# A decoder layer on one core: x1's turned tiles are sent and fetched ahead of x2's second tile, and x2 is read back in four transfers instead of eight

## The chip, the cores and the metric

The kernel runs on one core of a Trainium2 chip (TensorE, called PE below; VectorE, DVE; ScalarE, ACT; GpSimd, POOL; and SyncE, SP, which here only issues transfers). The metric is the device time of one execution in microseconds (us).

## The reference

A decoder layer on x of shape (2, 2048, 512) in f32, each of its three parts followed by a layer norm over the last axis:

```python
x = layernorm(x + self_attention(x))          # linear: no softmax, so it folds to x @ M + c
x = layernorm(x + cross_attention(x, ctx))    # 16 heads of 32, 154 context keys, masked softmax
x = layernorm(x + ffn(x))                     # mixes each token with the one before it
# ffn: xr = mu_r * x + (1 - mu_r) * x_prev ; xk likewise with mu_k
#      out = sigmoid(xr @ Wr.T) * (square(relu(xk @ Wk.T)) @ Wv.T)
```

Below, x1 is the result of the first layer norm and x2 that of the second.

## The kernel before

The 4096 tokens are worked in 16 groups of 256, each of two tiles of 128 tokens. Products in f32 precision are made of three matmuls (`three_pass`, L94 to L96), since each operand is split into a high and a low half. After a prologue that folds the self attention's weights into one matrix, a software pipeline runs over passes n. The steady loop has n = 2 to 14, and in pass n the engines work on four groups at once: a = n + 1 (y product, x1, q product), n (cross attention), f = n - 1 (output product, x2, mixing) and e = n - 2 (the ffn's k, r and v products). Each engine has its own list of instructions, written out by hand in the order in which it is to do them; semaphores (`flag`) tie the lists together, and an engine whose next instruction isn't released waits, whatever stands behind it.

PE's list for a pass (L2027 to L2059) is: k_product (e, 0), transposes (n, 0, t) with o_product (f, t), y_product (a, 0 and 1), values (n, 0), scores (n, 2), k_product (e, 1), transposes (n, 1, 0), r_product (e, 0), transposes (n, 1, 1), half of r_product (e, 1), values (n, 1), scores (n, 3), the other half, transposes (n, 2, 0), v_product (e, 0), transposes (n, 2, 1), q_product (a, 0) and so on. The numbers behind n are the head group (0 to 3) and the tile (0, 1). `values` (L1841) waits for `take_turned` and `take_rest` (L897, L902), with which ACT copies the transposed weights of attention out of PSUM; `transposes` (L1819) for the second tile waits for ACT's `take_turned` of the first.

x1 and x2 come out with tokens on partitions and must be turned so that features are on partitions. DVE turns squares of 32 x 32 in place (`turn_x2`, and inside `normalise_and_turn_x1`, both L1223), which gives the `x_squares` tiles; SP sends them to a scratch tensor in DRAM (L760, L774) and reads them back from there so that the squares land on the right partitions (`fetch_x1`, L766, four transfers; `fetch_x2`, L782, eight transfers, four for each tile). The two scratch tensors have 128 rows with the pieces of both tiles. Each layer norm takes its sums on DVE, `rstd` on POOL (`scale`, L1559, a power of -0.5) and is applied on DVE (L1201 for x2, L1232 for x1).

x1's way goes on as: ACT `x1_high` (L871), DVE `x1_low` (L1244), PE q_product (a, 0). x2's way goes on as: DVE `difference` (L1293), `blend`, and the products of the next pass. After its turning work DVE does `masked_min` (n, 2, 0), which takes the scores out of PSUM and finds the row's extreme (L1256); ACT's `exponentials` (n, 2, 0) (L889) wait for it, and on ACT there follow k_high, take_turned (n, 1, 1) and take_rest (n, 1):

```python
take_turned(n, 1, 0)
exponentials(n, 2, 0)
k_high(e, 1)
take_turned(n, 1, 1)
take_rest(n, 1)
```

Of the kernel before, what the change touches and what calls it, by code (L numbers as in the profile page):

```python
# [5 lines left out]
F32 = mybir.dt.float32  # L6
# [4 lines left out]
P = 128  # L11
B, S, D = 2, 2048, 512
KT = D // P
# [6 lines left out]
GT = 256  # L20
TPG = GT // P
# [9 lines left out]
SQUARE = 32  # L31
ROWS4 = P // SQUARE
# [581 lines left out]
def layers(nc, io, mem, tile, psum, weights, kv, m_in, xt, park, fold, out):  # L614
# [12 lines left out]
    m_park, c_park, x1_park, x2_park = park  # L627
# [7 lines left out]
    LAST = NG - 1  # L635
# [10 lines left out]
    with ExitStack() as ctx:  # L646
# [77 lines left out]
        end_mm, end_gated, end_sum, end_stat = (flag(x, len(parts)) for x in ("end_mm", "end_gated", "end_sum", "end_stat"))  # L724
        end_mom, end_var, end_rstd, end_ok = (flag(x, TPG) for x in ("end_mom", "end_var", "end_rstd", "end_ok"))
        x1_out, x1_back = flag("x1_out", TPG, 16), flag("x1_back", ROWS4, 16)
        x2_out, x2_back = flag("x2_out", TPG, 16), flag("x2_back", TPG * ROWS4, 16)

        x1_high_at, x1_low_at = (lambda n, ok=ok: ok.at(2, n) for ok in (x1t_hi_ok, x1t_lo_ok))

        def sp_program(sp):
            def load_mask(n):
                if n >= 2:
                    sp.wait_ge(*s_min.at(n - 2))
                sp.dma_start(mask_in[n % 2][:], io["mask"][n * GT:(n + 1) * GT, :]
                             .rearrange("(t p) c -> p t c", p=P)).then_inc(*mask_here.up)

            def load_x(n):
                sp.wait_ge(*q_mm.at(n - 1))
                sp.dma_start(x_in[:], x_cols[:, :, n * GT:(n + 1) * GT]).then_inc(*x_here.up)  # L740

            def load_batch(b):
                sp.wait_ge(*c_parked.at(0))
                sp.wait_ge(*m_parked.at(0))
                sp.wait_ge(*y_mm.at(b * GPB - 1))
                sp.dma_start(m_raw[:], m_park.rearrange("p (k n) -> p k n", k=KT)).then_inc(*m_here.up)
                sp.wait_ge(*y_sum.at(b * GPB - 1))
                sp.dma_start(c_row[:], c_park).then_inc(*c_here.up)

            def store(n):  # L750
                sp.wait_ge(*ln_ok[3].at(n))
                sp.dma_start(out[n * GT:(n + 1) * GT, :].rearrange("(t p) d -> p t d", p=P),
                             y3[:]).then_inc(*out_kept.up)

            def send_x1(n):
                for t in range(TPG):
                    sp.wait_ge(*tr1_mm.at(n, t + 1))
                    if n > 3:
                        sp.wait_ge(*x1_back.at(n - 4))
                    sp.dma_start(x1_park.rearrange("q (j t e) -> q t j e", j=ROWS4, t=TPG)[:, t],  # L760
                                 x1_squares[t][:].rearrange("q (j e) -> q j e", j=ROWS4)).then_inc(*x1_out.up)

            def fetch_x1(n):
                sp.wait_ge(*x1_out.at(n - 3))
                for j in range(ROWS4):
                    sp.dma_start(x_in[j * SQUARE:(j + 1) * SQUARE, :, :],  # L766
                                 x1_park.rearrange("(i r) (j e) -> j r i e", i=ROWS4, j=ROWS4)[j]).then_inc(*x1_back.up)

            def send_x2(n):
                for t in range(TPG):  # L770
                    sp.wait_ge(*tr2_mm.at(n, t + 1))
                    if n > 1:
                        sp.wait_ge(*x2_back.at(n - 2))
                    sp.dma_start(x2_park.rearrange("q (j t e) -> q t j e", j=ROWS4, t=TPG)[:, t],  # L774
                                 x2_squares[t][:].rearrange("q (j e) -> q j e", j=ROWS4)).then_inc(*x2_out.up)

            def fetch_x2(n, t):
                if t == 0:
                    sp.wait_ge(*x2_out.at(n - 1))
                    sp.wait_ge(*carried.at(n))  # L780
                for j in range(ROWS4):
                    sp.dma_start(x2t[j * SQUARE:(j + 1) * SQUARE, 1 + t * ROWS4:1 + (t + 1) * ROWS4, :, :],  # L782
                                 x2_park.rearrange("(i r) (j t k s) -> j t r i k s", i=ROWS4, j=ROWS4, t=TPG, k=KT)[j, t]
                                 ).then_inc(*x2_back.up)

            def load_weight(name):
                i = late.index(name)
                if i:
                    sp.wait_ge(*w_here.at(i - 1))
                sp.dma_start(raw[name][:], io[name].rearrange("(k p) n -> p k n", p=P)).then_inc(*w_here.up)  # L790

            def park(*parts):
                i, j = parts[0], parts[-1] + 1
                sp.wait_ge(*fm_eye.at(0, j))
                sp.dma_start(m_park.rearrange("p (k n) -> p k n", k=KT)[:, i:j, :], t1[:, i:j, :]).then_inc(*m_parked.up)

            load_mask(0)
            load_weight("ffn_wk")
            sp.dma_start(bo_row[:], io["rows"][4:5, :].broadcast_to([P, D])).then_inc(*bo_here.up)
            for n in range(-1, NG + 3):  # L800
                a, f, e = n + 1, n - 1, n - 2
                if n == 1:
                    sp.wait_ge(*fc_ok.at(0))
                    sp.dma_start(c_park, fold["c_row"][:]).then_inc(*c_parked.up)
                if live(e - 1) and e - 1 < LAST:
                    store(e - 1)
                if live(f) and moved_x2(f):
                    send_x2(f)
                if live(a) and moved_x1(a):
                    send_x1(a)  # L810
                if live(f) and moved_x2(f):
                    fetch_x2(f, 0)
                if live(a) and moved_x1(a):
                    fetch_x1(a)
                if live(f) and moved_x2(f):
                    fetch_x2(f, 1)
                if live(a) and a % GPB == GPB - 1 and a + 1 < NG:
                    load_batch(batch(a) + 1)
                if live(a + 1):
                    load_mask(a + 1)  # L820
                    if n == 1:
                        park(0, 1, 2)
                    load_x(a + 1)
                if n == 1:

                    sp.wait_ge(*fm_mm.at(0))
                    park(3)
                    load_weight("ffn_wr")
                    load_weight("ffn_wv")
            sp.wait_ge(*bo_here.at(0))  # L830
            for t in range(TPG):
                row = LAST * GT + t * P
                sp.wait_ge(*end_ok.at(0, t + 1))
                sp.dma_start(out[row:row + P, :], y3[:, t, :]).then_inc(*out_kept.up)
            sp.wait_ge(*out_kept.at(LAST - 1 + TPG))
# [288 lines left out]
        def dve_program(dve):  # L1124
# [325 lines left out]
            for n in range(2, LAST):  # L1450
                a, f, e = n + 1, n - 1, n - 2
                o_low(f, 3)
                masked_min(n, 1, 0)
                masked_min(n, 1, 1)
                k_square(e, 0)
                if a == GPB:
                    next_m_low(3)
                if live(e - 1):
                    normalise(3, e - 1, y3)
                o_finish(f, 0)  # L1460
                if n == 2:
                    weight_low("ffn_wr")
                else:
                    k_low(e, 0)
                o_finish(f, 1)
                if n == 2:
                    k_low(e, 0)
                normalise(2, f, x2[f % 2])
                y_finish(a, 0)
                turn_x2(f, 0)  # L1470
                y_finish(a, 1)
                o_low(n, 0)
                turn_x2(f, 1)
                normalise_and_turn_x1(a)
                masked_min(n, 2, 0)
                k_square(e, 1)
                masked_min(n, 2, 1)
                k_low(e, 1)
                if n == 2:
                    weight_low("ffn_wv")  # L1480
                make_mask(a)
                o_low(n, 1)
                masked_min(n, 3, 0)
                x1_low(a)
                masked_min(n, 3, 1)
                difference(f)
                v_gated(e, 0)
                blend(f, "k")
                v_sums(e, 0)
                o_low(n, 2)  # L1490
                k_mix_low(f)
                masked_min(a, 0, 0)
                masked_min(a, 0, 1)
                v_finish(e, 1)
                blend(f, "r")
                carry(f + 1)
                if a == GPB - 1:
                    next_m_low(0, 1, 2)
# [614 lines left out]
def decoder_layer(nc, whole, io, out):  # L2113
# [1 line left out]

    m_park = nc.dram_tensor("m_scratch", (P, KT * D), F32, kind="Internal").ap()
    c_park = nc.dram_tensor("c_scratch", (P, D), F32, kind="Internal").ap()
    x1_park, x2_park = (nc.dram_tensor(x + "_scratch", (P, TPG * D), F32, kind="Internal").ap() for x in ("x1", "x2"))
    mem = Map(nc)
    ident = mem.place("ident", [P, P])  # L2120
    ones = mem.place("ones", [P, P])
# [89 lines left out]
```

## Time and profile before

| | |
|---|---|
| median of 3 runs | 894.3 us (893.77 to 895.22) |
| the profiled execution | 892.91 us, of which the span of the profile is 890.8 us |
| PE matmul busy | 875.6 us, 98% of the span |
| PE weight loads busy | 727.9 us, 82% |
| DVE busy | 711.5 us, 80% |
| ACT busy | 534.0 us, 60% |
| POOL busy | 499.5 us, 56% |
| TensorE clock granted | 0.999 of full |

All times in the profile are counted from the span's start. An engine's timeline gives for each instruction its start, its duration, the engine, the line of the kernel (a helper's line where a helper issues it), what it writes and reads and, in brackets, how long the engine had been idle before it and what released it. Neighbouring instructions of one engine overlap at their ends, so the distance between two starts is what one costs. The x load at the end of each pass (L740) marks the passes: pass 3 reaches from 262.83 to 308.12.

### The profile page before, as it was taken

The numbers are of one execution on the slowest core, as the hardware profiler recorded it, in microseconds if no ns is written. First come the engines' busy times: TensorE is split into PE (matmuls) and PEld (weight loads), VectorE is DVE, ScalarE is ACT, GpSimd is POOL, SyncE is SP. The second block draws the span as 40 slices with busy tenths as digits, with TensorE's granted clock in tenths as the row PEclk, the third lists the DMA queues.
The fourth block names the chain that finished last, engine by engine and source line by source line (L and its number), as shares of the span: only waits on it lengthen the run. The fifth ranks groups of instructions, "written<-read, shape, count | busy, mean of one in ns | idle before, by whom it ended". The sixth has DMA issues, their size and how long they took to land.

```text
span 890.8 us, 23143 instructions
## 1 busy us (share of the span) xinstructions
PE 875.6 (98%) x8566; PEld 727.9 (82%) x8566; DVE 711.5 (80%) x2053; ACT 534.0 (60%) x1631; POOL 499.5 (56%) x505
## 2 busy tenths in 40 slices
PE   9999999999999999999999999999999999999997
PEld 8877867778788888888888888888888888888786
DVE  6688566576898888888797878787978887977775
ACT  7555425858565757474757574757565666666631
POOL 1035014676776565666666667575757666666420
PEclk9999999999999999999999999999999999999999
DMA  9792020103412222222422222313131313130001
GB/s 293 249 276 72 24 74 26 44 2 127 126 50 88 64 82 67 80 59 87 118 79 71 72 80 66 86 61 91 61 92 57 95 50 103 48 97 25 2 24 47
DMA packets 82252, 73.80 MB, mean 83 GB/s; under 512 B 7134, under 2 KB 66526, under 8 KB 82014
## 3 DMA queue, kind: packets, MB, share of 16 engines
q1 hardware_dynamic: 78542, 65.27, 24.2%
q10 hardware_dynamic: 3600, 7.08, 2.4%
q8 instruction: 68, 1.11, 0.5%
q14 instruction: 42, 0.34, 0.1%
HBM read 47.73 MB, written 23.33 MB: 80 GB/s over the span
## 4 chain that ended last, share of the span: by engine, by line
PE 64%; POOL 8%; issue 7%; DVE 6%; ACT 1%; DMA 1%; POOLq 0%; DVEq 0%
PE dense L94 17%; PE dense L95 16%; PE dense L96 16%; PE turned L1819 5%; PE turned L1841 5%; PE scores L1805 4%; POOL row_inv L1572 2%; POOL weight L1580 2%; PE turned L1823 1%; POOL prob_rest L1579 1%; DVE stats L1188 1%; POOL x L1590 1%; POOL rstd L1559 1%; DVE x_squares L1223 1%; DMA xt_raw<-x_cols 1%
## 5 line engine op out<-in xcount | busy, mean ns | idle before, releaser
L1572 POOL TENSOR_TENSOR row_inv<-row_sum,minus_one 128x4 f32<-128x4 f32 x128 | 143.8, 1123 | 161.9 <-ACT prob L889 160.4
L889 ACT ACTIVATE prob<-prob,row_min 128x154 f32<-128x154 f32 x512 | 209.5, 416 | 17.2 <-DVE row_min L1256 17.1
L1580 POOL TENSOR_TENSOR weight<-prob,row_inv 128x512 f32<-128x512 f32 x128 | 141.0, 1102 | 0.0
L1256 DVE CUSTOM_DVE_ANT_0 prob<-scores,mask_add 128x154 f32<-128x154 f32 x512 | 128.3, 311 | 3.9 <-PE scores L1805 3.6
L897 ACT ACTIVATE prob_t<-turned 128x512 f32<-128x512 f32 x128 | 75.4, 589 | 52.5 <-PE turned L1819 52.4
L889 ACT ACTIVATION_READ_ACCUMULATOR prob<-prob,row_min 128x1 f32 x512 | 98.5, 192 | 0.0
L1819 PE MATMUL turned<-ident,weight 128*128 128x128 f32 x512 | 77.0, 273 | 2.5 <-DVE o_t_lo L1263 1.1
L94 PE MATMUL dense<-xt_hi,cross_wq_hi 128*128 128x256 f32 x256 | 76.6, 299 | 0.2 <-ACT u L846 0.2
L1819 PEld LDWEIGHTS turned<-ident,weight 128*128 128x128 f32 x512 | 61.1, 140 | 18.0 <-issue 4.1
L94 PE MATMUL dense<-mix_k_hi,ffn_wk_hi 128*128 128x256 f32 x256 | 75.1, 293 | 0.0
L95 PE MATMUL dense<-xt_lo,cross_wq_hi 128*128 128x256 f32 x256 | 73.1, 286 | 0.0
L96 PE MATMUL dense<-xt_hi,cross_wq_lo 128*128 128x256 f32 x256 | 72.6, 284 | 0.0
L910 ACT ACTIVATE o_t_hi<-turned 128x256 fp32r<-128x256 f32 x64 | 24.0, 375 | 80.3 <-PE turned L1841 80.3
L95 PE MATMUL dense<-mix_k_lo,ffn_wk_hi 128*128 128x256 f32 x256 | 71.9, 281 | 0.0
L96 PE MATMUL dense<-mix_k_hi,ffn_wk_lo 128*128 128x256 f32 x256 | 71.9, 281 | 0.0
L1559 POOL TENSOR_TENSOR rstd<-var,neg_half 128x2 f32<-128x2 f32 x47 | 35.5, 756 | 59.7 <-DVE var L1195 58.0
L1590 POOL TENSOR_TENSOR x<-x,cross_bo_row 128x1024 f32<-128x1024 f32 x16 | 38.4, 2400 | 38.2 <-DVE x_squares L1223 34.5
L1263 DVE TENSOR_TENSOR o_t_lo<-turned,o_t_hi 128x256 fp32r<-128x256 f32 x64 | 26.8, 419 | 40.0 <-ACT o_t_hi L910 39.8
L1579 POOL TENSOR_TENSOR prob_rest<-prob,row_inv 128x104 f32<-128x104 f32 x128 | 50.5, 394 | 10.0
L94 PE MATMUL dense<-cross_wo_hi,o_t_hi 128*128 128x512 f32 x128 | 53.1, 415 | 0.0
L94 PEld LDWEIGHTS dense<-mix_k_hi,ffn_wk_hi 128*128 128x128 f32 x256 | 48.2, 188 | 4.9 <-issue 4.8
L1805 PE MATMUL scores<-kt,q 32*128 32x154 f32 x1024 | 51.6, 315 | 0.0
(283 smaller groups left out, 2640.5 us busy)
## 6 DMA issues: line engine op xcount, KB each, us to landing
x_scratch<-x_squares SPq DMA_DIRECT2D x52, 256.0 KB, 2.6
x_rows<-x_rows SPq DMA_DIRECT2D x32, 256.0 KB, 4.2
xt_raw<-x_cols SPq DMA_DIRECT2D x16, 512.0 KB, 3.8
out<-gate_then_y SPq DMA_DIRECT2D x15, 512.0 KB, 2.8
x_t<-x_scratch SPq DMA_DIRECT2D x104, 64.0 KB, 2.4
xt_raw<-x_scratch SPq DMA_DIRECT2D x52, 128.0 KB, 2.8
mask_in<-mask SPq DMA_DIRECT2D x16, 154.0 KB, 2.3
cross_wv<-cross_wv SPq DMA_DIRECT2D x2, 512.0 KB, 5.3
```

Of the source, the lines that this page charges most:

```text
L94: pe.matmul(out, sta[0], mov[0], start=first, stop=False, skip_group_check=True)
L95: pe.matmul(out, sta[0], mov[1], start=False, stop=False, skip_group_check=True)
L96: return pe.matmul(out, sta[1], mov[0], start=False, stop=last, skip_group_check=True)
L889: m = act.activation(keys, keys, ACT.Exp, bias=row_min[:, buf, t, h:h + 1], scale=-1.0, accum_out=row_sum[:, buf, t, h:h + 1])
L897: act.activation(pt[:, 0:HPG, t * P:(t + 1) * P], t_bank[:].rearrange("p (c n) -> p c n", c=HPG), ACT.Copy).then_inc(*t_out.up)
L1256: m = dve.tensor_tensor_reduce(exp_slot(n, u)[:, i * CTX:(i + 1) * CTX], s_bank[:, h, t * CTX:(t + 1) * CTX], mask_add[n % 2][:, t, :], -S ...
L1572: pool.tensor_tensor(row_inv[:, buf, t, :], row_sum[:, buf, t, :], minus_one[:], ALU.pow).then_inc(*p_inv.up)
L1579: pool.tensor_tensor(after, late, inv_late, ALU.mult)
L1580: pool.tensor_tensor(first, early, inv_early, ALU.mult).then_inc(*p_norm.up)
L1590: pool.tensor_tensor(rows[:], rows[:], bo_row[:].unsqueeze(1).broadcast_to([P, TPG, D]), ALU.add).then_inc(*x1_bo.up)
L1805: m = pe.matmul(s_bank[:, h, t * CTX:(t + 1) * CTX], q[rows, g, t * P:(t + 1) * P], kt[rows, g, b * CTX:(b + 1) * CTX], start=True, stop=T ...
L1819: m = pe.transpose(t_bank[:, i * P:(i + 1) * P], weight_slot(n, u)[:, i * P:(i + 1) * P], ident[:])
```

## The change

`normalise_and_turn_x1(a)` now stands ahead of `turn_x2(f, 1)` in DVE's list. SP's list for a pass was: both tiles of x2 sent, both tiles of x1 sent, x2's first tile fetched (4 transfers), x1 fetched (4), x2's second tile fetched (4). It is now: x2's first tile sent, both tiles of x1 sent, x2's second tile sent, x1 fetched (4), x2 fetched, both tiles in each of 4 transfers of 128 KB. The scratch tensor of x2 has now a row for each token, so that each tile is sent as 128 rows of 2 KB in one piece instead of 128 x 4 pieces of 512 bytes; the reads still take pieces of 512 bytes.

```diff
-        x2_out, x2_back = flag("x2_out", TPG, 16), flag("x2_back", TPG * ROWS4, 16)
+        x2_out, x2_back = flag("x2_out", TPG, 16), flag("x2_back", ROWS4, 16)
...
-            def send_x2(n):
-                for t in range(TPG):
-                    sp.wait_ge(*tr2_mm.at(n, t + 1))
-                    if n > 1:
-                        sp.wait_ge(*x2_back.at(n - 2))
-                    sp.dma_start(x2_park.rearrange("q (j t e) -> q t j e", j=ROWS4, t=TPG)[:, t],
-                                 x2_squares[t][:].rearrange("q (j e) -> q j e", j=ROWS4)).then_inc(*x2_out.up)
-
-            def fetch_x2(n, t):
-                if t == 0:
-                    sp.wait_ge(*x2_out.at(n - 1))
-                    sp.wait_ge(*carried.at(n))
+            def send_x2(n, t):
+                sp.wait_ge(*tr2_mm.at(n, t + 1))
+                if n > 1:
+                    sp.wait_ge(*x2_back.at(n - 2))
+                sp.dma_start(x2_park[t * P:(t + 1) * P, :], x2_squares[t][:]).then_inc(*x2_out.up)
+
+            def fetch_x2(n):
+                sp.wait_ge(*x2_out.at(n - 1))
+                sp.wait_ge(*carried.at(n))
                 for j in range(ROWS4):
-                    sp.dma_start(x2t[j * SQUARE:(j + 1) * SQUARE, 1 + t * ROWS4:1 + (t + 1) * ROWS4, :, :],
-                                 x2_park.rearrange("(i r) (j t k s) -> j t r i k s", i=ROWS4, j=ROWS4, t=TPG, k=KT)[j, t]
-                                 ).then_inc(*x2_back.up)
+                    sp.dma_start(x2t[j * SQUARE:(j + 1) * SQUARE, 1:, :, :].rearrange("r b k s -> r b (k s)"),
+                                 x2_park.rearrange("(b r) (j e) -> j r b e", r=SQUARE, j=ROWS4)[j]).then_inc(*x2_back.up)
...
-                if live(f) and moved_x2(f):
-                    send_x2(f)
-                if live(a) and moved_x1(a):
+                if 2 <= n < LAST:
+                    send_x2(f, 0)
                     send_x1(a)
-                if live(f) and moved_x2(f):
-                    fetch_x2(f, 0)
-                if live(a) and moved_x1(a):
+                    send_x2(f, 1)
                     fetch_x1(a)
-                if live(f) and moved_x2(f):
-                    fetch_x2(f, 1)
+                    fetch_x2(f)
...
                 turn_x2(f, 0)
                 y_finish(a, 1)
                 o_low(n, 0)
+                normalise_and_turn_x1(a)
                 turn_x2(f, 1)
-                normalise_and_turn_x1(a)
                 masked_min(n, 2, 0)
...
-    x1_park, x2_park = (nc.dram_tensor(x + "_scratch", (P, TPG * D), F32, kind="Internal").ap() for x in ("x1", "x2"))
+    x1_park, x2_park = (nc.dram_tensor(x + "_scratch", shape, F32, kind="Internal").ap() for x, shape in (
+        ("x1", (P, TPG * D)), ("x2", (GT, D))))
```

## Rows read from the trace of the kernel before

**Rows 1.** Windows of passes 3 and 10: length, each engine's busy us, clock, DMA.

```profile
262.83:308.12 45.29, 45.29 (x496) 38.47 (x503) 38.28 (x120) 28.34 (x94) 29.44 (x31) 1.00 0.25 75
...
580.58:626.02 45.44, 45.44 (x496) 38.37 (x504) 37.83 (x119) 28.24 (x94) 29.44 (x30) 1.00 0.26 75
```

**Rows 2.** PE's waits from 232 to 810 us: total us, times, longest.

```profile
PE turned L1819 <- DVE o_t_lo L1263: 1.1, 2, 0.6
PE turned L1841 <- ACT prob_t L902: 0.9, 1, 0.9
PE dense L94 <- DVE square L1316: 0.4, 1, 0.4
```

**Rows 3.** Timeline of DVE, pass 3.

```profile
276.84 1.00 DVE L1201 TENSOR_SCALAR x<-x,moments,rstd 128x512 f32<-128x512 f32 x2 [0.81 <-POOL rstd L1559]
...
281.96 0.70 DVE L1223 STREAM_TRANSPOSE x_squares<-x 128x512 f32<-128x512 f32 x1
282.61 0.55 DVE L1232 TENSOR_SCALAR x<-x,moments,rstd 128x512 f32<-128x512 f32 x1
...
295.51 1.19 DVE L1293 TENSOR_TENSOR mix_r_raw<-x_t 128x992 f32<-128x992 f32 x1
```

**Rows 4.** Timeline of POOL, pass 3.

```profile
276.10 0.70 POOL L1559 TENSOR_TENSOR rstd<-var,neg_half 128x2 f32<-128x2 f32 x1 [3.26 <-DVE var L1195]
...
281.80 0.70 POOL L1559 TENSOR_TENSOR rstd<-var,neg_half 128x2 f32<-128x2 f32 x1
```

**Rows 5.** Timeline of ACT, pass 3.

```profile
286.04 0.42 ACT L889 ACTIVATE prob<-prob,row_min 128x154 f32<-128x154 f32 x1 [0.69 <-DVE row_min L1256]
...
288.68 0.36 ACT L902 ACTIVATE prob_t<-turned 128x256 f32<-128x256 f32 x1
...
292.32 1.06 ACT L871 ACTIVATE xt_hi<-xt_raw 128x1024 fp32r<-128x1024 f32 x1 [0.90 <-DMA xt_raw<-x_scratch]
```

**Rows 6.** Timeline of PE, pass 3: values (1) and transposes (2, 1).

```profile
289.45 0.67 PE L1841 MATMUL turned<-prob_t,v_first 64*32 64x128 f32 x32
...
295.77 0.60 PE L1819 MATMUL turned<-ident,weight 128*128 128x128 f32 x4
```

**Rows 7.** Timelines of ACT and PE, pass 2, then pass 12.

```profile
240.24 0.42 ACT L889 ACTIVATE prob<-prob,row_min 128x154 f32<-128x154 f32 x1 [2.58 <-DVE row_min L1256]
...
242.88 0.36 ACT L902 ACTIVATE prob_t<-turned 128x256 f32<-128x256 f32 x1
...
243.38 0.67 PE L1841 MATMUL turned<-prob_t,v_first 64*32 64x128 f32 x32 [0.86 <-ACT prob_t L902]
...
697.26 0.37 ACT L902 ACTIVATE prob_t<-turned 128x256 f32<-128x256 f32 x1
...
697.94 0.67 PE L1841 MATMUL turned<-prob_t,v_first 64*32 64x128 f32 x32
```

**Rows 8.** Timelines of ACT and PE, pass 10.

```profile
611.47 1.06 ACT L871 ACTIVATE xt_hi<-xt_raw 128x1024 fp32r<-128x1024 f32 x1 [2.27 <-DMA xt_raw<-x_scratch]
...
612.91 0.59 ACT L897 ACTIVATE prob_t<-turned 128x512 f32<-128x512 f32 x1
...
613.64 0.63 PE L1819 MATMUL turned<-ident,weight 128*128 128x128 f32 x4
```

**Rows 9.** Timeline of SP's transfers, pass 3 (x2: several issues in one row).

```profile
283.93 1.69 SPq L760 DMA_DIRECT2D x_scratch<-x_squares  x2
...
287.83 1.82 SPq L766 DMA_DIRECT2D xt_raw<-x_scratch  x4
```

**Rows 10.** x1's sends and x1's reads over the run: issue ns, time to landing.

```profile
L760 SPq DMA_DIRECT2D x_scratch<-x_squares x26: 512/513/776, 238.1 to 784.2; - x26
...
DMA to landing us min/median/max: 2.6/2.7/3.7
...
L766 SPq DMA_DIRECT2D xt_raw<-x_scratch x52: 302/432/438, 242.0 to 788.3; - x52
...
DMA to landing us min/median/max: 2.5/2.8/4.4
```

## The prediction

> **What bounds the kernel now.** After the page I read the table by windows, cut at the start of each x load, so that a window is one pass of the steady loop (the one from 262.83 is pass n = 3). It shows that PE is simply full: a pass takes 45.29 us, all of it busy, at the full clock, while DVE, the next busiest, works 38 us of it [rows 1]. So nothing is bought by an engine or a transfer that gets quicker beside PE; only a wait of PE can be taken away, and only one that reaches PE can be added. The list of PE's waits over all thirteen passes of the loop that the change touches (n = 2 to 14) has four, 2.4 us in sum, three of them in pass 2 [rows 2]. A fifth shows only in a window's length: pass 10 takes 45.44 us instead [rows 1].
>
> The question is then how near each engine stands to PE at the places that are moved. For that I read the engines' timelines of one pass, n = 3, and compare each finish with the PE instruction that waits for it.
>
> **DVE: the moved transpose.** Before, DVE turns x2's second tile at 281.96 and normalises and turns x1 from 282.61 on; the score tiles of group 2 follow [rows 3]. The new order puts that transpose behind x1's. Its slot is 0.65 us (282.61 - 281.96), and the last x1 transpose, behind which it comes, has the same shape. The slot wasn't free time: x1's normalisation needs POOL's rstd, which is only there at 281.80 + 0.70 = 282.50 [rows 4]. From such a wait DVE starts 0.04 us later (276.10 + 0.70, then 276.84) [rows 3, 4], so x1 can start at 282.54, only 0.07 us earlier, with DVE idle in front of it where the transpose had covered POOL. Behind x1 the transpose costs its slot in full: the score tiles start 0.65 - 0.07 = 0.58 us later, and I take 0.57, as the other transposes of the pass are 0.64 apart from what follows.
>
> **What waits for the score tiles.** ACT's exponentials of tile (2, 0) had waited 0.69 us for the first of them, and from their start at 286.04 ACT works without a gap: four exponentials, k_high, take_turned (1, 1), take_rest, which ends at 288.68 + 0.36 = 289.04 [rows 5]. PE's values (1) waits for take_rest and starts at 289.45 [rows 6], 0.41 us later. From a finish on ACT to a start on PE that had waited for it takes 0.14 us: in pass 2 take_rest ends at 243.24 and values (1) starts at 243.38, as its wait of 0.86 us shows [rows 7], and pass 10 gives the same (612.91 + 0.59 = 613.50, then 613.64) [rows 8]. So the free slack is only 0.41 - 0.14 = 0.27 us, and the delay is 0.57. PE stalls 0.30 us in pass 3. Over the twelve passes 3 to 14 the gap is 0.31 us (pass 12, in [rows 7]) to 0.43, 4.63 us in sum; 12 x (0.57 + 0.14) - 4.63 = 3.89 us.
>
> Nothing gives it back. PE has no idle time after it in the pass, and the chain itself hangs on PE (o_finish waits for PE's o product), so the next pass starts with the same distance and stalls again. In pass 2 values (1) already waits on this same chain, and its exponentials waited 2.58 us for DVE [rows 7], so there the full 0.57 us comes on top. Other work behind the score tiles is late by the same 0.57 us: k_square for the second half of r_product, the second score tile for scores (3), o_low (1) for transposes (2, 0). Where one of these reaches PE too it takes the place of a part of the same stall: one delayed chain can hold PE back by no more than 0.57 us in a pass, 13 x 0.57 = 7.4 us in all, which is the upper bound. The lower one is nothing, if the delay is under 0.27.
>
> **SP: the transfers.** Removed are 4 issues a pass, 52 in all, of 0.43 us; SP isn't on PE's path. Before, x1's fetch is issued at 287.83, between the two halves of x2's [rows 9]. Now it stands ahead of them, but it waits for x1's second send. That send was issued at 283.93 + 1.69 - 0.51 = 285.11 [rows 9] and now goes at 285.04; such sends land after 2.6, 2.7 or 3.7 us (least, median, most) [rows 10], so the fetch starts at 287.74: the first four x2 issues had covered just the time of the landing. The order gives x1 0.09 us, and perhaps 0.3 more as it isn't queued behind x2's reads. Its first user is ACT's x1_high at 292.32 [rows 5]. What PE feels of x1 is the take_turned (2, 0) that stands behind it on ACT: from x1_high to the transposes (2, 1) that wait takes 613.64 - 611.47 = 2.17 us in pass 10 [rows 8], against 295.77 - 292.32 = 3.45 us in pass 3 [rows 6, 5]. So x1 has 1.28 us to spare in pass 3, and being earlier brings nothing except in pass 10, where it takes back 45.44 - 45.29 = 0.15 us [rows 1].
>
> x2's second send moves from some 282.7 (281.96 + 0.70) to 285.7, one transpose behind x1's second send: ahead of x1's fetch in the queue but inside the wait for x1's landing, so nothing behind it is held. The merged reads follow x1's four (1.82 us [rows 9]) from 289.6 on, when x2's send has landed even with 3.7 us (289.4), and the last is issued at about 287.74 + 1.82 + 1.82 - 0.43 = 290.95. Reads of their size, 128 KB, land after 2.5, 2.8 or 4.4 us [rows 10]: x2 is there at 293.4 to 295.4, and DVE's difference reads it at 295.51 [rows 3]. Covered, by 0.1 us even at the slowest, and without the cover it would delay DVE's difference, blend and gated product, not PE at once. The mask and x loads behind the reads come no later, as SP is through with its issues at 291.4. I take 0 for the transfers; the bounds are the two rivals' prices below.
>
> A rule speaks against merging: the Trainium skill, Perfetto Trace Analysis, section DMA Optimizations, says that smaller pieces may let some of a transfer start sooner. The trace doesn't bear it out here, since already the first of the eight reads waited for both tiles' sends; by the rule or by the row the sum stays the same.
>
> **Sum.** 0.57 + 3.89 - 0.15 = +4.3 us. On the profiled execution's own 892.91 us that is 897.2; the median of the runs shown, 894.3, lies 1.4 above it, and I forecast on the median: 898.6, of which I round off 0.1 for x1 landings that may be late in ordinary runs. Forecast 898.5 us, 0.5% slower. Its own range: with 0.47 instead of 0.57 us of delay in all thirteen passes it is 897.2, with 0.67 it is 899.8.
>
> **Rivals.** About 0.2% (1.8 us) is what a measurement of this kernel can tell from no change.
>
> No change, 894.3 (893 to 896). It decides at 0.27 us: if the delay of the score tiles is below that, PE never waits. For it speaks that 0.57 rests on POOL's rstd being the next thing late, and POOL's spans are rough; were rstd ready 0.3 us sooner, the delay would be 0.27. Against it: another wait for POOL's rstd shows 0.04 us between finish and start [rows 3, 4], so its spans fit, and even without any 0.14 us of signal the stall would be 12 x 0.57 - 4.63 + 0.57 = 2.8 us. Chance 0.18.
>
> Faster, 891.8 to 892.5. The place is PE's transposes (2, 1), behind x1_high and take_turned (2, 0). The ordinary runs are 0.9 to 2.3 us above the profiled one; if that is x1 landing late in some passes, as in pass 10, an earlier and freer x1 removes it. The most that there is to gain in the passes are PE's waits, 2.4 + 0.15 = 2.5 us, from 894.3. It needs the 0.57 us to be hidden as well, so it decides at the same 0.27. The Trainium skill, DMA: Bandwidth & Descriptors, Rules for kernel authors, would favour it: many small transfers should be coalesced, under 64 KB one pays mostly overhead. The trace agrees that the bytes count for little, as a send of 256 KB lands in 2.7 us and a read of 128 KB in 2.8 [rows 10], but that time lies beside PE. Chance 0.08.
>
> Slower still, 900.5 to 902. x1's fetch now stands bare on its send's landing. If that is 3.7 us instead of 2.7 and the reads slow with it, x1_high moves past the 1.28 us of slack; 0.3 us over it in twelve passes would be 3.6 us on top. Against it: the 3.7 is the longest of 26 sends, and 1 us is less than the 1.28 to spare. Chance 0.08.
>
> **How the numbers follow.** Forecast 0.66. All of it, and the last rival, are slower by over 0.2% (0.74); same 0.18; faster 0.08. The range 894.8 to 900.2 takes the forecast with its own range, the upper part of no change and the edge of the slowest; it leaves out about 0.2.
>
> **What will show it.** Right: on PE a wait of values (1) for take_rest (or ACT) of about 0.3 us in each of twelve passes and about 1.4 in pass 2; passes of 45.6 us; DVE idle for POOL's rstd before L1232, some 0.5 us; exponentials (2, 0) 0.57 us later behind the o product. x1's fetch about 0.1 us earlier only. Wrong: passes still of 45.29 us, or a wait on PE at the q product or at transposes (2, 1) instead, or DVE idle before the difference for x2.

## The result and the profile after

The changed kernel takes 898.62 us (median of 4 runs, 897.49 to 899.06) against 894.03 us (4 runs, 893.07 to 895.22). The ratio is 1.0052, with a 95% interval from 1.0039 to 1.0065: slower by half a per cent. The profiled execution is 897.49 us with a span of 895.5, 4.7 more than before. Two executions stand alone far outside of all others (4847.6 us, the first one of e3 below, and 1419.64 us, one of the kernel before beside e5 to e7) and are left out of the comparisons.

First the windows of passes 3, 7 and 10 after, cut as before at the x loads (length, then busy us of PE, its weight loads, DVE, ACT, POOL), and below them PE's waits over the whole loop:

```profile
263.49:309.15 45.66, 45.38 (x496) 38.50 (x504) 38.81 (x120) 28.53 (x94) 29.91 (x31) 1.00 0.27 74
...
446.03:492.36 46.33, 45.52 (x496) 38.49 (x504) 40.01 (x124) 29.53 (x96) 30.32 (x31) 1.00 0.27 73
583.63:629.28 45.65, 45.37 (x496) 38.48 (x503) 38.78 (x120) 28.48 (x94) 29.86 (x31) 1.00 0.27 74
```

```profile
PE turned L1833 <- ACT prob_t L894: 4.3, 13, 0.9
PE turned L1811 <- DVE o_t_lo L1255: 1.1, 2, 0.6
PE dense L94 <- DVE square L1308: 1.0, 1, 1.0
```

A pass is 0.37 us longer than in [rows 1], and PE is no longer full: in every one of the thirteen passes it waits at values (1) for ACT's take_rest, 4.3 us in sum, where before there was one such wait [rows 2]. The line numbers are 8 lower from the change on. Pass 7, which is longer in both kernels, grew alike, from 46.00 to 46.33. Pass 10 grew only from 45.44 to 45.65, about 0.15 less than the others: no read of x1 landed later than 3.7 us in this execution, where the slowest had taken 4.4 before [rows 10].

Now pass 3 on each engine. DVE and POOL, at the place that was moved:

```profile
282.29 0.42 DVE L1255 TENSOR_TENSOR o_t_lo<-turned,o_t_hi 128x256 fp32r<-128x256 f32 x1
283.27 0.55 DVE L1224 TENSOR_SCALAR x<-x,moments,rstd 128x512 f32<-128x512 f32 x1 [0.56 <-POOL rstd L1551]
...
285.03 1.31 DVE L1215 STREAM_TRANSPOSE x_squares<-x 128x512 f32<-128x512 f32 x2
286.26 0.28 DVE L1248 CUSTOM_DVE_ANT_0 prob<-scores,mask_add 128x154 f32<-128x154 f32 x1
```

```profile
282.46 0.70 POOL L1551 TENSOR_TENSOR rstd<-var,neg_half 128x2 f32<-128x2 f32 x1
```

DVE has nothing left to do for 0.56 us until rstd is there; that is the slot which x2's second transpose had filled in [rows 3]. The transpose now stands as the second of the pair at 285.03, and the score tiles begin behind it. ACT and PE:

```profile
284.92 0.60 ACT L911 ACTIVATE relu<-dense 128x512 f32<-128x512 f32 x1 [3.36 <-PE dense L96]
...
287.30 0.43 ACT L881 ACTIVATE prob<-prob,row_min 128x154 f32<-128x154 f32 x1 [1.29 <-DVE row_min L1248]
...
289.94 0.36 ACT L894 ACTIVATE prob_t<-turned 128x256 f32<-128x256 f32 x1
...
292.75 1.07 ACT L863 ACTIVATE xt_hi<-xt_raw 128x1024 fp32r<-128x1024 f32 x1
```

```profile
290.45 0.67 PE L1833 MATMUL turned<-prob_t,v_first 64*32 64x128 f32 x32 [0.28 <-ACT prob_t L894]
```

ACT's idle time before the exponentials has grown from 0.69 us [rows 5] to 1.29, so they come 0.60 us later behind PE's work. take_rest ends at 290.30, and PE starts 0.15 us after it, from a real wait of 0.28 us. x1_high starts at 292.75, only 0.07 us after ACT is free (292.09 + 0.59, gate_then_y), so x1 and ACT are ready at nearly the same time here; in six of the thirteen passes ACT still waits for x1's reads, 2.2 us in all.

SP's issues in pass 3, and the landings of x1's sends and of the merged x2 reads over the run:

```profile
284.59 1.70 SPq L760 DMA_DIRECT2D x_scratch<-x_squares  x2
286.38 0.58 SPq L773 DMA_DIRECT2D x_scratch<-x_squares  x1
288.38 1.75 SPq L766 DMA_DIRECT2D xt_raw<-x_scratch  x4
290.23 1.85 SPq L779 DMA_DIRECT2D x_t<-x_scratch  x4
```

```profile
L760 SPq DMA_DIRECT2D x_scratch<-x_squares x26: 512/524/625, 238.2 to 788.5; - x26
...
DMA to landing us min/median/max: 2.6/2.6/3.2
...
L779 SPq DMA_DIRECT2D x_t<-x_scratch x52: 302/450/1618, 243.9 to 794.4; - x52
...
DMA to landing us min/median/max: 3.1/3.6/4.7
```

From the start of the pass, x1's fetch goes at 288.38 - 263.49 = 24.89 us, against 287.83 - 262.83 = 25.00 [rows 9]: 0.11 us earlier. Its first send goes at 284.59 - 263.49 = 21.10 us, as before (283.93 - 262.83).

### The profile page after: what moved, and what is told of

Same layout as the page of the kernel before. It is cut to its first block, busy times and chain, and to the rows that moved or that the text cites. A ratio compares the mean times of both kernels' runs of the same rounds, so it can differ in the third digit from the quotient of the medians.

```text
span 895.5 us, 23091 instructions
## 1 busy us (share of the span) xinstructions
PE 876.0 (98%) x8566; PEld 728.1 (81%) x8566; DVE 716.6 (80%) x2053; ACT 535.9 (60%) x1631; POOL 502.8 (56%) x505
## 4 chain that ended last, share of the span: by engine, by line
POOL 30%; issue 19%; PE 19%; DVE 13%; ACT 2%; DMA 2%; POOLq 1%; DVEq 0%
POOL row_inv L1564 9%; POOL weight L1572 8%; PE dense L94 4%; PE dense L96 4%; PE dense L95 4%; POOL prob_rest L1571 3%; POOL rstd L1551 3%; POOL xt_lo L1544 3%; DVE x_squares L1215 3%; POOL x L1582 3%; DVE stats L1180 3%; DVE x L1201 2%; DMA xt_raw<-x_cols 2%; DVE x L1193 2%; PE turned L1811 2%
## 5 line engine op out<-in xcount | busy, mean ns | idle before, releaser
L1564 POOL TENSOR_TENSOR row_inv<-row_sum,minus_one 128x4 f32<-128x4 f32 x128 | 146.0, 1140 | 163.4 <-ACT prob L881 162.8
```

The source lines that it names most:

```text
L1564: pool.tensor_tensor(row_inv[:, buf, t, :], row_sum[:, buf, t, :], minus_one[:], ALU.pow).then_inc(*p_inv.up)
```

## The experiments

Theory A is that of the prediction: DVE's moved transpose makes the score tiles of group 2 late by 0.6 us, and PE's values (1) has 0.27 us of slack. Theory B, the rival, lays the loss to the transfers. Theory C, a second rival, lets any delay on DVE cost what it lasts. All of the ratios below are against the kernel before, run on the same chip with them (893.38 us for e1 to e4, 893.37 for e5 to e7).

| run | median us | ratio | 95% interval |
|---|---|---|---|
| e1, transfers only | 893.23 | 1.0002 | 0.9993 to 1.001 |
| e2, DVE's order only | 915.15 | 1.0244 | 1.0227 to 1.0261 |
| e3, transpose behind the score tiles | 893.6 | 1.0004 | 0.9995 to 1.0013 |
| e3b, e3 once more for its profile | 894.38 (one run) | | |
| e4, score tiles first | 893.45 | 1.0004 | 0.9995 to 1.0013 |
| e5, 0.14 us of delay | 893.95 | 1.0004 | 0.9995 to 1.0013 |
| e6, 0.57 us of delay | 897.74 | 1.0046 | 1.0032 to 1.0059 |
| e7, 1.16 us of delay | 906.11 | 1.0136 | 1.012 to 1.0152 |

A ratio is estimated from all compared executions, so it isn't exactly the quotient of the two medians.

**e1: the transfers alone.** The changed kernel with DVE's old order:

```diff
                 o_low(n, 0)
-                normalise_and_turn_x1(a)
                 turn_x2(f, 1)
+                normalise_and_turn_x1(a)
                 masked_min(n, 2, 0)
...
                     send_x2(f, 0)
-                    send_x1(a)
                     send_x2(f, 1)
+                    send_x1(a)
                     fetch_x1(a)
                     fetch_x2(f)
```

> The changed SP list and scratch layout (2 KB sends, x1 fetched ahead of x2, x2 in four reads) with DVE's order of before; both x2 sends go ahead of x1's, as DVE turns them so. Theory A (the 0.6 us by which DVE's moved transpose delays the score tiles of group 2 is more than the 0.27 us of slack at PE's values (1)): no such delay here, so as before, 893.4 to 894.7 us, passes of 45.29 us, no wait at values (1) in passes 3 to 14. Theory B (the loss comes from the transfers: x1's fetch bare on its send's landing, or the larger x2 reads): the whole +4.6 us, about 898.6.

893.23 us, no change, and PE's waits are those of before (those of [rows 2], and one of 0.3 us ahead of 232 us, which the kernel before has too):

```profile
PE turned L1811 <- DVE o_t_lo L1255: 1.1, 2, 0.6
PE turned L1833 <- ACT prob_t L894: 0.9, 1, 0.9
PE dense L94 <- DVE square L1316: 0.4, 1, 0.4
PE dense L94 <- DVE x L1261: 0.3, 1, 0.3
```

Theory B falls. Four reads instead of eight, sends in pieces of 2 KB and x1's fetch ahead of x2's neither cost nor bring anything.

**e2: DVE's order alone.** The kernel before with one edit:

```diff
                 o_low(n, 0)
+                normalise_and_turn_x1(a)
                 turn_x2(f, 1)
-                normalise_and_turn_x1(a)
                 masked_min(n, 2, 0)
```

> The kernel before with DVE's order changed alone: normalise_and_turn_x1 ahead of turn_x2 (f, 1); SP's list and the scratch as before. Theory A: at least the whole loss, 898.6, with PE's wait at values (1) of about 0.3 us in each pass; as SP still wants x2's second tile before it sends x1, x1 comes some 1.5 us later, which about uses up its 1.28 us of slack, so up to 900.5. Theory B: 894.0, or a loss that stands at transposes (2, 1) or the q product alone and not at values (1).

915.15 us, 21.8 more, far over what either theory had said. PE waits in two places:

```profile
PE turned L1819 <- ACT prob_t L897: 12.7, 13, 2.0
PE turned L1841 <- ACT prob_t L902: 4.7, 13, 0.9
```

The second line is the change's own loss. The first is x1 being late: SP still waited for x2's second tile before it sent x1, and then issued x2's first four reads, which wait for that tile's landing, ahead of x1's. In pass 3:

```profile
288.42 1.30 SPq L760 DMA_DIRECT2D x_scratch<-x_squares  x2
290.44 1.80 SPq L782 DMA_DIRECT2D x_t<-x_scratch  x4
292.36 1.78 SPq L766 DMA_DIRECT2D xt_raw<-x_scratch  x4
```

```profile
296.72 1.06 ACT L871 ACTIVATE xt_hi<-xt_raw 128x1024 fp32r<-128x1024 f32 x1 [2.59 <-DMA xt_raw<-x_scratch]
```

The pass starts at 264.95, so x1's fetch is issued at 27.41 us of the pass instead of 25.00, and x1_high starts at 31.77 instead of 29.49, 2.28 us later. Of that 1.28 was to spare and 0.35 is the stall at values (1) just before; the remaining 0.65 us stalls transposes (2, 1) behind take_turned (2, 0) on ACT. I had expected x1 1.5 us later because I left out that wait of x2's first reads for the second tile's landing. Pass 3 is one of the cheaper ones: it takes 46.33 us, 1.04 more than before, but from pass 6 on there are passes of up to 47.87 (pass 11). There SP takes 3.31 us for x1's four reads instead of 1.78, and PE waits 2.0 us at transposes (2, 1). So about 1 us a pass makes only some 14 us of the 21.8, pass 2 included; the rest is x1 coming later still in those passes, and why its reads are slower there isn't shown. So the way by which late transfers could have hurt is real; it is the new SP order of the change that keeps x1 clear of it.

**e3: the transpose one place further back.**

```diff
                 normalise_and_turn_x1(a)
-                turn_x2(f, 1)
                 masked_min(n, 2, 0)
+                turn_x2(f, 1)
```

> The changed kernel with x2's second transpose one place further back, behind masked_min (n, 2, 0). x1 still goes first, the transfers are those of the change. Theory A: the score tiles start no later than before, the waits of about 0.3 us at values (1) go in passes 3 to 14, and the time is that of before, 893.4 to 894.8; k_square and the second score tile are still 0.6 us late, which reaches PE in pass 2 at most. Theory B: x1 and x2 travel as in the change (x2 a little later), so 898.6 or more.

893.6 us: the whole loss is gone with x1 still first and all of the new transfers. The same kernel was profiled once more, in a run of its own (e3b):

> The kernel of e3 once more, for its profile. Theory A: PE's waits in passes 3 to 14 are gone at values (1), passes of 45.3 us, and the exponentials (2, 0) start 1.8 us after relu's start, as before, instead of 2.4 in the change; k_square 0.6 us later than before costs PE nothing after pass 2.

```profile
286.56 0.43 ACT L881 ACTIVATE prob<-prob,row_min 128x154 f32<-128x154 f32 x1 [0.71 <-DVE row_min L1248]
```

```profile
PE turned L1833 <- ACT prob_t L894: 0.7, 3, 0.3
PE turned L1811 <- ACT prob_t L889: 0.7, 1, 0.7
```

```profile
296.88 1.19 DVE L1285 TENSOR_TENSOR mix_r_raw<-x_t 128x992 f32<-128x992 f32 x1 [0.71 <-DMA x_t<-x_scratch]
```

ACT's idle time is back at 0.71 us, and ten of the thirteen waits at values (1) are gone; three are left, in passes 2, 11 and 13, 0.7 us in all. Those in 11 and 13 I had not expected: the exponentials had waited 1.17 and 1.31 us for the score tiles there, so DVE itself was late, and what made it so isn't shown. (The profiled execution of e6 has one such pass too, 11, with 0.86 us instead of 0.28.) The last line of the three fences shows what moved instead: x2's second tile is sent later still, and DVE's difference now waits 0.71 us for the merged reads. That reaches no PE instruction of its own.

The wait of transposes (2, 1), 0.7 us, stands in pass 9. There one of x1's reads took 5.2 us to land, the slowest of the 52, and ACT and PE waited for it:

```profile
567.35 1.06 ACT L863 ACTIVATE xt_hi<-xt_raw 128x1024 fp32r<-128x1024 f32 x1 [3.02 <-DMA xt_raw<-x_scratch]
```

```profile
569.53 0.63 PE L1811 MATMUL turned<-ident,weight 128*128 128x128 f32 x4 [0.72 <-ACT prob_t L889]
```

So x1's reads can still land late, and cost PE time, with x1 fetched first.

**e4: the score tiles ahead of x1.**

```diff
                 o_low(n, 0)
+                masked_min(n, 2, 0)
                 normalise_and_turn_x1(a)
                 turn_x2(f, 1)
-                masked_min(n, 2, 0)
```

> The changed kernel with masked_min (n, 2, 0) ahead of normalise_and_turn_x1, where DVE would idle for POOL's rstd; x1 starts about 0.3 us later, x2's second transpose behind it. Theory A: the exponentials start 0.7 us earlier than before (then bound by ACT's own list), the slack at values (1) grows from 0.27 to about 0.9 us, and pass 2 loses part of its 0.86 us wait: 892.9 to 894.3. Theory B: x1 and x2 are both later than in the change, so 898.6 or more.

893.45 us. Now the 0.95 us of score tiles fill DVE's wait for rstd, and ACT's exponentials start with no idle time at all:

```profile
285.01 0.43 ACT L881 ACTIVATE prob<-prob,row_min 128x154 f32<-128x154 f32 x1
```

```profile
PE turned L1811 <- DVE o_t_lo L1255: 1.5, 2, 0.9
PE dense L94 <- DVE square L1308: 0.3, 1, 0.3
PE dense L94 <- DVE x L1261: 0.3, 1, 0.3
PE turned L1811 <- ACT prob_t L889: 0.3, 1, 0.3
```

The wait of values (1) is gone even in pass 2, but 0.4 us of it came back as a longer wait for o_low (1.5 instead of 1.1 us in two) and 0.3 at transposes (2, 1). Making the slack bigger buys nothing: it was enough that it isn't used up.

**e5, e6, e7: a delay by itself.** The kernel before, with an instruction that computes nothing that is used, between x1's turning and the score tiles. x1, x2 and all transfers stay as they were:

```diff
                 turn_x2(f, 1)
                 normalise_and_turn_x1(a)
+                dve.bn_stats(ones[:, 0:6], bo_row[:, 0:96])     # e5; 0:512 in e6 and e7; in e7 also the next line
+                dve.bn_stats(ones[:, 6:12], bo_row[:, 0:512])
                 masked_min(n, 2, 0)
```

> The kernel before with one small extra instruction on DVE (bn_stats over 96 columns into unused columns) between x1's turning and masked_min (n, 2, 0); it computes nothing that is used. It should take some 0.2 us. Theory A: that is under the 0.27 us of slack at values (1), so no stall in passes 3 to 14 and 893.4 to 894.0 us. Theory C (a delay of DVE costs what it lasts, wherever it is, 13 x 0.2): 896.0.

> The same with the extra instruction over 512 columns, some 0.61 us, as much as the change delays the score tiles by; transfers, x1 and x2 exactly as before. Theory A: PE waits about 0.34 us at values (1) in twelve passes and 0.6 more in pass 2, +4.7 us, 898.1, the same as the change. Theory B (transfers): 893.4. Theory C: 13 x 0.61 = +7.9, 901.3.

> The same with two extra instructions over 512 columns, some 1.22 us. Theory A: 12 x (1.22 - 0.27) + 1.22 = +12.6 us, 906.0, still nearly all of it at values (1). Theory C: 13 x 1.22 = +15.9, 909.3.

The extra instruction of e5 and the score tile behind it, then that of e6; from start to start they are 0.14 and 0.57 us, and in e7 the two are 1.16:

```profile
284.93 0.22 DVE L1475 BATCH_NORM_STATS2 ones<-cross_bo_row 128x6 f32<-128x96 f32 x1
285.07 0.30 DVE L1256 CUSTOM_DVE_ANT_0 prob<-scores,mask_add 128x154 f32<-128x154 f32 x1
```

```profile
285.85 0.65 DVE L1475 BATCH_NORM_STATS2 ones<-cross_bo_row 128x6 f32<-128x512 f32 x1
286.42 0.30 DVE L1256 CUSTOM_DVE_ANT_0 prob<-scores,mask_add 128x154 f32<-128x154 f32 x1
```

PE's waits at values (1) in e6, then those in e7:

```profile
PE turned L1842 <- ACT prob_t L902: 4.8, 13, 0.9
```

```profile
PE turned L1843 <- ACT prob_t L902: 11.1, 13, 0.9
PE dense L94 <- DVE square L1316: 2.1, 2, 1.6
```

By theory A the times are 893.37 + 0.14 = 893.5 (the delay reaches PE in pass 2 alone), 893.37 + 12 x (0.57 - 0.27) + 0.57 = 897.5, and 893.37 + 12 x (1.16 - 0.27) + 1.16 = 905.2; measured were 893.95, 897.74 and 906.11. Theory C with the same delays gives 895.2, 900.8 and 908.4. So e5 and e6 fit A, and e7 lies 0.9 us above A and 2.3 below C; at values (1) each of the passes 3 to 14 of e7 loses what A says (11.1 us with pass 2), and k_square's waits, 2.1 us in two, in passes 2 and 13, where before it was 0.4 in one, show that so long a delay reaches a second place too. Passes 7 and 13 grow the most, to 47.26 us (46.00 before) and 46.98 (45.32 before), the others to 46.2 to 46.4. e5's interval ends at 1.0013, 1.2 us, which leaves out C's 1.8. e6 makes the loss of the change without touching the order of x1 and x2 or any transfer.

## Why the prediction came out

Right, in its mechanism and its size: 898.5 us was forecast and 898.62 measured. That the two lie within 0.12 us is in part luck, as the points on the median, on pass 10 and on the moved transpose show.

- **The moved transpose.** It had filled DVE's wait for POOL's rstd, and DVE now idles there for 0.56 us, as forecast (some 0.5). The delay of the score tiles was forecast at 0.57 us and is 0.60 (ACT's idle time 1.29 instead of 0.69). Two errors of that sum nearly cancel. DVE starts x1 0.11 us after rstd's end (282.46 + 0.70 = 283.16, then 283.27), not 0.04 after it as the prediction had taken from another wait; 0.11 is the distance that it had before too [rows 3, 4], so the 0.07 us that the sum took back in front weren't there. And the transpose costs less than its slot of 0.65 us behind x1: the pair takes 286.26 - 285.03 = 1.23 us to the first score tile, where one alone took 0.64, so 0.59.
- **The slack and the stall.** From ACT's end to PE's start it is 0.15 us (forecast 0.14). Apart from pass 10, passes 3 to 13 are 0.31 to 0.37 us longer, pass 3 by 0.37; forecast were 0.30 in pass 3 and 0.32 on average, and the difference is about that of the delay. e6 shows the slack from the other side.
- **Pass 2.** There 0.57 us was forecast, and the pass is 0.60 us longer (263.49 - 207.86 against 262.83 - 207.80, from x load to x load). But the sign that was named for it, about 1.4 us at values (1), didn't come: that wait stayed at 0.9, and the one for k_square grew from 0.4 to 1.0 instead. The prediction had allowed for that in its working (one stall takes the place of another), not in its signs.
- **Pass 10.** It got back the 0.15 us of its late x1 (45.65 instead of the 45.8 that its own 45.44 and the others' growth would make). That the order did this isn't shown: e1, with x1 fetched first too, still has a read of x1 that takes 4.4 us, and e3b one that takes 5.2 and costs PE 0.7 us.
- **Transfers.** x1's fetch was forecast 0.09 us earlier and goes 0.11 earlier, and it does wait for its send's landing, where it had been covered by four of x2's issues. But the 0.07 us that x1's turning was to give aren't in it, as the sends stand where they stood in the pass; they landed a little sooner, in 2.6 us instead of 2.7 at the median. e1 gives 0 for all of the transfers, as the sum had it. What was wrong without consequence is the landing of the merged reads: I took 2.8 us from reads of the same size, and it is 3.6, up to 4.7. DVE's difference waits for them in no pass, as x1_low and all behind it on DVE run later too.
- **The rivals.** No change was to decide at 0.27 us of delay: e5, under it, shows no loss and e6, over it, does. Faster fell with e1 and e4, where the delay was absent and the time still that of before: being first in the queue doesn't free x1 of late landings, as e1 and e3b show. Whether such landings are what separates ordinary runs from the profiled one stays open; e3b, 894.38 us, has one that costs 0.7. Slower still didn't come in the change, but its mechanism did in e2, at the place named, transposes (2, 1).

The median lies 4.6 us above that of before; the working gave 4.3 for the trace and the profiled executions differ by 4.58 (897.49 - 892.91). The delay, 0.03 us larger in thirteen passes, so +0.4, is about the difference. The forecast itself was helped by its base: it stood on 894.3, the median of three runs before, and with the fourth that became 894.03.

No version tried beats the kernel before: e1, e3, e4 and it can't be told apart, because PE is all but full in all four of them.

## What to carry to other kernels

When one engine is full for whole passes, work on the others is worth nothing until it eats the last slack to an instruction of the full engine; find that slack by comparing each releaser's end with the start of the instruction it releases, and take off the delay from signal to start, before any order is changed. An instruction that seems to stand in the way of a more urgent one may be filling a wait for a third engine, and then moving it back costs nearly its full slot behind and, here, gained nothing in front. And a transfer moved forward in a queue gets no earlier than what it waits for: look at what had covered that wait.

## What the runs showed of the hardware

- Reads of 128 KB landed at different times: x1's, in pieces of 1 KB, after 2.8 us (median), x2's merged ones, in pieces of 512 bytes, after 3.6. As x2's also stand behind x1's in the queue, it isn't shown that the pieces make the difference. The issue of a send in pieces of 2 KB takes SP 0.34 us where nothing was issued just before it, and 0.58 right behind x1's second send (both in the fence above); sends in pieces of 512 bytes take 0.51 to 0.52 at the median.
- DVE's x1_low, 1.22 to 1.23 us long in every pass before, took 1.62 us in the median in the changed kernel. In pass 3 it ran from 293.85 on while POOL worked on a weight tile from 293.41; in e1, e2 and e4, where x1_low in pass 3 meets POOL for 0.02 us at most, the median is again 1.23 us. The overlap in pass 3 is 0.60 us and x1_low takes 0.46 us longer; in e6 it is 0.41 us (294.23 to 294.64) and x1_low takes 1.49 us, 0.26 longer. In all eleven passes of the changed kernel in which the weight tile is first and overlaps (by 0.16 to 0.69 us) x1_low takes longer by the overlap less 0.14 to 0.15 us, and e6 and e7 give the same figure with overlaps up to 0.79. In pass 2 it is the other way round: x1_low is first and keeps its 1.22 us, and POOL's weight tile takes 2.06 us instead of 1.04, with 1.15 us of overlap. So whichever of the two starts second seems to stand still until the first is through, apart from that 0.14 us. That is read from the overlaps and wasn't tried by itself. The Trainium skill, Perfetto Trace Analysis, section Optimizing Scalar/DVE Operations, says that GpSimd and DVE share an SBUF read port, which would fit.

```profile
L1236 DVE TENSOR_TENSOR xt_lo<-xt_raw,xt_hi x13: 1210/1621/1767, 248.6 to 796.6; 128x1024 fp32r<-128x1024 f32 x13
```

```profile
293.41 1.04 POOL L1572 TENSOR_TENSOR weight<-prob,row_inv 128x512 f32<-128x512 f32 x1
```

- From ACT's end to PE's start it took 0.14 to 0.15 us in each of the thirteen passes of the changed kernel at values (1), where PE always waited.
